# Layer 0's recurrence: one logistic operation per job, and half of the products with B on GpSimd

## The chip, the core and the metric

The kernel runs on one core of a Trainium2 chip. Its engines work from queues of their own and meet at semaphores: TensorE (PE in the rows; PEld is its weight load), VectorE (DVE), ScalarE (ACT), GpSimd (POOL) and SyncE (SP, which starts transfers). Each queue is strictly in order: an instruction that waits holds up all behind it. [...] The metric is the device time of one execution in microseconds (us), the median of several runs.

## The reference

The program is a tower of four layers over 32 images of 50 tokens with 192 features. The change lies in the mixer of layer 0, a bilinear state-space recurrence with 16 states per feature (shortened):

```python
A = -jnp.exp(A_log)                      # 192 features x 16 states
bc = x @ W_bc                            # B_sel, C_sel: 16 columns each
delta = softplus(x @ W_dt @ W_dtp + b_dt)
delta = soft_clamp(delta * rsqrt(mean(delta**2) + 1e-6) * rms_scale, 1e-4, 10.0)
half  = 0.5 * delta[..., None] * A
denom = 1.0 - half
A_bar = (1.0 + half) / denom
Bx    = sqrt(delta)[..., None] * B_sel[:, :, None, :] / denom * x_in[..., None]
h_t   = A_bar_t * h_{t-1} + Bx_t         # over the 50 tokens of an image
y     = sum over states of C_sel * h + D_param * x
```

With r = 1/denom, a number between 0 and 1, the decay A_bar is 2r - 1. denom is 1 + 0.5 exp(A_log) delta, so r is also the logistic function of -(ln delta + A_log - ln 2).

## The kernel before

The stage works on features in partitions and tokens along the free dimension. The 1600 tokens are cut into 4 chunks of 400, the turns of a loop (`CHUNKS`). The 192 x 16 pairs of feature and state are cut into 24 jobs a chunk (`JOBS0`): two jobs of three hold 128 features of one state, the third holds the remaining 64 features of two states, which two copies side by side fill to 128 rows. A job is thus 128 rows of 400 tokens, float32.

The work of a job j, in `bilinear_scan`, is shared out so:

- TensorE spreads the row of B over 128 partitions into a bank of PSUM (`spread_b`, line 558, two banks that alternate), does the same with C (`spread_c`, line 558), and adds the result of a job to the sum over states (`add`, line 575, with the identity, or with the folded identity for the third kind of job). Its order is spread_b(j+1), spread_c(j), add(j-2).
- ScalarE computes ln(1 + coef x rate) (`logarithm`, line 600), then its exponential with a minus sign, r (`invert`, line 607), then the decay 2r - 1 into PSUM (`decay`, line 613). Its order is logarithm(j), invert(j-1), decay(j-2). There are two buffers of decays, so that decay(j) waits for the scan of job j-2.
- GpSimd multiplies the input with r (line 633), into `w1`.
- VectorE multiplies `w1` with the spread row of B from PSUM (`weigh`, line 650, into `w2`), scans over the tokens (`recur`, line 656), and multiplies the states with the spread row of C (`read`, line 662). Its order is weigh(j), read(j-1), recur(j). At a chunk's end it writes y (line 675).

All this is written out by hand as the order of each engine's instructions; there is no planner. Four slots of each buffer (`SLOTS`) and semaphores that count jobs keep the engines apart. Ahead of the loop `split_thirds` splits B and C into three bfloat16 parts, on VectorE (lines 501 to 509), as a block of its own: blocks are parted by a barrier of all engines. Layer 3 has a scan of its own (`scan`, from line 680). There B's row goes from PSUM into SBUF on ScalarE (line 821) and GpSimd does the product with it (line 850); the lines 742 (add), 746 (spread), 805 (decay), 875 (scan) and 881 (read) belong to it.

The lines that set TensorE's order:

```python
spread_b(0)
for j in range(jobs):
    if j + 1 < jobs:
        spread_b(j + 1)
    spread_c(j)
    if j >= 2:
        add(j - 2)
```

The functions that the change touches, as they are before it:

Of the kernel before, what the change touches and what calls it, by code (L numbers as in the profile page):

```python
# [489 lines left out]
def split_thirds(t, bc, thirds, select, select_pair):  # L490

    nc = t.nc
    with ExitStack() as inner:
# [3 lines left out]
        with t.block() as block:  # L497
            @block.vector
# [22 lines left out]
def bilinear_scan(t, u, rate, coef, bc, direct, gain, y):  # L521
# [5 lines left out]
    jobs = JOBS0  # L527
    group = lambda j: job_states(j)[0]
    with ExitStack() as st:
# [3 lines left out]
        split_thirds(t, bc, thirds, select, select_pair)  # L533
        names = ("den_done", "r_done", "a_done", "w1_done", "w2_done", "s_done", "g_done", "summed", "b_spread", "c_spread", "y_done", "a_zero")
        (den_done, r_done, a_done, w1_done, w2_done, s_done, g_done, summed, b_spread, c_spread, y_done, a_zero) = (t.sem(n) for n in names)
        w2, s, g_, den, r, w1 = (t.sbuf(n, [128, SLOTS, CHUNK], st) for n in ("w2", "s", "g", "den", "r", "w1"))
# [7 lines left out]
        with t.block() as block:  # L544
            @block.tensor
            def _(pe):
                pe.sem_inc(summed, SLOTS)
                pe.wait_ge(fold_done, 1)
                with pe.Fori(0, CHUNKS) as c:
# [10 lines left out]
                    def spread_b(j):  # L560
                        pe.wait_ge(w2_done, c * jobs + j - 1 + SLOTS)
                        pe.sem_inc(t.passed, 1)
                        spread_row(bankB[j % 2], j, 0).then_inc(b_spread, 1)
# [61 lines left out]
            def _(pool):  # L625
                pool.sem_inc(w1_done, SLOTS)
# [1974 lines left out]
```

## Time and profile before

| what | value |
|---|---|
| median of 3 runs | 2521.09 us (2516.54 to 2526.69) |
| the profiled execution | 2526.45 us, its span 2524.6 us |
| TensorE busy | 2005.6 us, 79% of the span |
| VectorE busy | 1189.0 us, 47% |
| ScalarE busy | 890.3 us, 35% |
| GpSimd busy | 843.8 us, 33% |
| mean granted clock | 0.859 |

The shares are means over stages with different limits; layer 0's recurrence, from about 205 to 397 us, is one of them. The span is the time from the first to the last instruction of the one execution whose trace is read. In rows of the order of time the first two numbers are start and duration in us; the square brackets say how long the engine was idle before and what ended that. Durations of one engine's neighbours overlap a little, so that the distance from start to start is what an instruction costs its engine.

### The profile page before, as it was taken

To read this page: it belongs to the slowest core of one execution; us is meant where nothing else is said; L and a number is where in the kernel's file an instruction comes from. 1 tells how busy PE (TensorE), PEld (TensorE's weight loads), DVE (VectorE), ACT (ScalarE), POOL (GpSimd) and SP (SyncE) were. 2 spreads that over 40 slices of the span, in tenths; PEclk is the share of its full clock that TensorE was granted. 3 is DMA by queue.
4 is the path that set the end of the run, shared out by engine and by line. 5 is a ranking of instruction groups with operands and counts; after the bars stand their busy time and mean duration, and the time that the engine had idled before them with its cause. 6 is when DMAs were issued, how large, how long until landed. Compare 5 with 4: busy or idle time off the path is not lost. (4 is left out here: it accounts for less than half of the span.)

```text
span 2524.6 us, 42132 instructions
## 1 busy us (share of the span) xinstructions
PE 2005.6 (79%) x13338; PEld 1484.1 (59%) x13338; DVE 1189.0 (47%) x2907; ACT 890.3 (35%) x1860; POOL 843.8 (33%) x759
## 2 busy tenths in 40 slices
PE   9755777987995994985995567777499938999998
PEld 8511223665764883664983222224399837999987
DVE  4348995243563113563113799998222243222222
ACT  1247784133233332342224644553222122211211
POOL 0203552012111553001552267663234312443443
PEclk9757997876896995895997789999599957999999
DMA  7100000000004871003871000000377626777774
GB/s 217 31 0 1 0 0 1 0 0 6 1 0 122 237 206 35 1 0 106 225 205 26 0 1 0 0 0 1 113 223 221 170 69 191 224 222 224 221 201 113
DMA packets 95935, 228.18 MB, mean 90 GB/s; under 512 B 22481, under 2 KB 60948, under 8 KB 87540
## 3 DMA queue, kind: packets, MB, share of 16 engines
q1 hardware_dynamic: 64564, 188.81, 23.4%
q0 software_dynamic: 31296, 38.48, 8.4%
q8 instruction: 34, 0.56, 0.1%
q14 instruction: 41, 0.34, 0.0%
HBM read 199.63 MB, written 27.62 MB: 90 GB/s over the span
## 5 line engine op out<-in xcount | busy, mean ns | idle before, releaser
L1964 PE MATMUL banks<-wt,hid 128*128 128x192 f32 x1932 | 331.7, 327 | 0.4
L1964 PEld LDWEIGHTS banks<-wt,hid 128*128 128x128 f32 x1932 | 311.8, 190 | 1.5 <-issue 0.6
L1866 POOL DMA_INDIRECT xblock<-table,take x169 | 167.6, 992 | 370.7 <-DVE gate L2149 193.8
L1939 PE MATMUL banks<-xTblock,wt 128*128 128x256 f32 (+1 forms) x1464 | 268.6, 341 | 1.7 <-ACT xTblock L2022 1.2
L2162 DVE TENSOR_TENSOR hid<-sa,banks 128x512 f32<-128x512 f32 (+1 forms) x183 | 105.9, 579 | 340.1 <-ACT sa L2043 337.3
L2043 ACT ACTIVATE sa<-banks 128x512 f32<-128x512 f32 (+1 forms) x183 | 93.3, 510 | 481.5 <-PE banks L1950 476.6
L1939 PEld LDWEIGHTS banks<-xTblock,wt 128*128 128x128 f32 x1464 | 237.6, 194 | 23.7 <-issue 1.9
L742 PE MATMUL banks<-g,consts 128*128 128x400 f32 x384 | 184.7, 571 | 60.1 <-DVE g L881 56.1
L850 POOL TENSOR_TENSOR w<-u,spreadB 128x400 f32<-128x400 f32 x192 | 192.9, 1034 | 87.0 <-ACT spreadB L821 87.0
L1871 POOL DMA_INDIRECT sums<-yblock,put x96 | 152.7, 1591 | 170.5 <-issue 98.6
L875 DVE TENSOR_TENSOR_SCAN s<-banks,w 128x400 f32<-128x400 f32 x192 | 187.7, 977 | 4.2 <-POOL w L850 4.2
L2177 DVE TENSOR_SCALAR yblock<-banks,gate 128x192 f32<-128x192 f32 x129 | 49.4, 414 | 235.2 <-PE banks L1964 204.3
L742 PEld LDWEIGHTS banks<-g,consts 128*128 128x128 f32 x384 | 61.0, 197 | 168.4 <-DVE g L881 167.2
L633 POOL TENSOR_TENSOR w<-u,r 128x400 f32<-128x400 f32 x96 | 99.0, 1033 | 175.4 <-ACT r L607 163.4
L805 ACT ACTIVATE banks<-rate,coef 128x392 f32 x192 | 113.2, 591 | 117.8 <-DVE s L875 117.8
L1950 PE MATMUL banks<-xTblock,wt 64*128 64x256 f32 (+1 forms) x1464 | 143.3, 342 | 0.0
L1871 POOL DMA_INDIRECT out<-yblock,put x65 | 103.6, 1594 | 115.0 <-issue 56.5
L1950 PEld LDWEIGHTS banks<-xTblock,wt 64*128 64x128 f32 x1464 | 116.1, 187 | 22.9 <-issue 12.1
L881 DVE TENSOR_TENSOR g<-s,banks 128x400 f32<-128x400 f32 x192 | 103.3, 540 | 0.0
L1943 PE MATMUL banks<-xTblock,wt 128*128 128x256 f32 (+1 forms) x480 | 94.7, 349 | 2.2 <-ACT xTblock L2022 1.3
L656 DVE TENSOR_TENSOR_SCAN s<-banks,w 128x400 f32<-128x400 f32 x96 | 93.8, 977 | 0.1
L1926 PE MATMUL banks<-consts,xblock 128*128 128x128 f32 x338 | 61.5, 296 | 38.7 <-DMA xblock<-table,take 38.6
(379 smaller groups left out, 3455.5 us busy)
## 6 DMA issues: line engine op xcount, KB each, us to landing
wt<-L3f_packed SPq DMA_DIRECT2D x41, 1152.0 KB, 5.6
wt<-L_packed SPq DMA_DIRECT2D x60, 576.0 KB, 4.6
wt<-L3f_packed SPq DMA_DIRECT2D x41, 576.0 KB, 5.4
wt<-L3m_packed SPq DMA_DIRECT2D x20, 1152.0 KB, 5.4
wt<-L_packed SPq DMA_DIRECT2D x20, 675.0 KB, 4.2
wt<-L3m_packed SPq DMA_DIRECT2D x20, 577.0 KB, 5.4
pixels<-pixels SPq DMA_DIRECT2D x16, 375.0 KB, 4.8
wshift<-w_patch SPq DMA_DIRECT2D x8, 450.0 KB, 11.9
```

The source lines that it names most:

```text
L633: nc.gpsimd.tensor_tensor(w1[:, j % SLOTS, :], u[:, group(j), at], r[:, j % SLOTS, :], ALU.mult).then_inc(w1_done, 1)
L742: nc.tensor.matmul(acc[g][0:parts, 0:CHUNK], ident[0:parts, 0:parts], g_[:, j % SLOTS, :], start=(n == 0), stop=(n == STATES - 1)).then_in ...
L805: nc.scalar.activation(rest, rate[:, g, at].rearrange("p (b t) -> p b t", t=SEQ)[:, :, 1:SEQ], ACT.Exp, scale=coef[:, g, n:n + 1]).then_in ...
L850: nc.gpsimd.tensor_tensor(w2[:, j % SLOTS, :], u[:, g, at], spreadB[:, n % 2, :], ALU.mult).then_inc(bu_done, 1)
L875: nc.vector.tensor_tensor_scan(s[:, j % SLOTS, :], decays[j % DECAYS], w2[:, j % SLOTS, :], 0.0, ALU.mult, ALU.add).then_inc(s_done, 1)
L881: nc.vector.tensor_tensor(g_[:, j % SLOTS, :], s[:, j % SLOTS, :], bankC[(j // groups) % 2][0:parts, 0:CHUNK], ALU.mult).then_inc(g_done, 1)
L1866: nc.gpsimd.indirect_dma_start(x[:, b % 2, q - column_of_block[b], :], None, table, bass.IndirectOffsetOnAxis(take[:, q:q + 1], 0)).then_i ...
L1871: nc.gpsimd.indirect_dma_start(sums, bass.IndirectOffsetOnAxis(put[:, q:q + 1], 0), y[:, b % 2, q - column_of_block[b], :], None, compute_ ...
L1939: nc.tensor.matmul(bank[:, n * j:n * (j + 1)], wt[:, v, cols(base, 2 * p + j)], xT[:, v, 0, 0:n], start=(j == 0), stop=False, skip_group_c ...
L1950: last = nc.tensor.matmul(bank[:, n * j:n * (j + 1)], wt[half, v, cols(REST_AT, 2 * p + j)], xT[half, v, 1, 0:n], start=False, stop=True, ...
L1964: last = nc.tensor.matmul(bankY[s], hid[:, m, 128 * s:128 * (s + 1)], wt[:, v, DOWN_AT + DIM * m:DOWN_AT + DIM * (m + 1)], start=(m == 0 a ...
L2162: nc.vector.tensor_tensor(hid[:, 2 * p:2 * p + 2, 0:n], sa[:, (PAIRS * v + p) % 2, 0:2 * n].rearrange("p (m n) -> p m n", m=2), second[:, ...
```

## The change

Ahead of the loop, in the block of `split_thirds`, ScalarE replaces rate by its logarithm (four operations on 128 x 800). Per job, Ln and Exp are replaced by one logistic operation on that logarithm, with the scale -1 and a bias for each feature and state; `coef` now holds this bias, and the Exp that made `coef` is gone. The buffer `den` is gone. For odd jobs ScalarE copies the spread row of B from PSUM to SBUF (`spreadB`, two buffers), and GpSimd multiplies `w1` with it, behind the input's product of the next job. For even jobs VectorE multiplies as before. The semaphore `w2_done` becomes `even_weighed` and `odd_weighed`; `b_copied` counts the copies. TensorE's order is as before, but the spread of an odd row waits for the copy of the odd row before it.

```diff
+            @block.scalar
+            def _(act):
+                nc.scalar.preload_act_table_set("natural_log_exp_and_others")
+                for c in range(CHUNKS):
+                    at = slice(CHUNK * c, CHUNK * (c + 1))
+                    nc.scalar.activation(rate[:, :, at], rate[:, :, at], ACT.Ln)
+                nc.scalar.preload_act_table_set("sigmoid_and_others")
...
-                        pe.wait_ge(w2_done, c * jobs + j - 1 + SLOTS)
+                        if by_pool(j):
+                            pe.wait_ge(b_copied, c * HALVES + j // 2 + 1)
+                        else:
+                            pe.wait_ge(even_weighed, c * HALVES + j // 2 + SLOTS // 2)
...
-                for sem in (den_done, r_done, a_done):
+                for sem in (r_done, a_done):
                     act.sem_inc(sem, SLOTS)
-                nc.scalar.preload_act_table_set("natural_log_exp_and_others")
+                act.sem_inc(b_copied, 1)
...
-                    def logarithm(j):
-                        act.wait_ge(r_done, c * jobs + j + 1)
-                        act.sem_inc(t.passed, 1)
-                        nc.scalar.activation(den[:, j % SLOTS, :], rate[:, group(j), at], ACT.Ln,
-                                             scale=coef[:, j:j + 1], bias=1.0).then_inc(den_done, 1)
-
-                    def invert(j):
-                        act.wait_ge(den_done, c * jobs + j + 1 + SLOTS)
+                    def share(j):
                         act.wait_ge(a_done, c * jobs + j + 1)
                         act.wait_ge(w1_done, c * jobs + j + 1)
-                        nc.scalar.activation(r[:, j % SLOTS, :], den[:, j % SLOTS, :], ACT.Exp, scale=-1.0).then_inc(r_done, 1)
+                        act.sem_inc(t.passed, 1)
+                        nc.scalar.activation(r[:, j % SLOTS, :], rate[:, group(j), at], ACT.Sigmoid,
+                                             scale=-1.0, bias=coef[:, j:j + 1]).then_inc(r_done, 1)
+
+                    def copy_b(j):
+                        act.wait_ge(b_spread, c * jobs + j + 1)
+                        act.wait_ge(odd_weighed, c * HALVES + j // 2 + 1)
+                        nc.scalar.activation(spreadB[:, j // 2 % 2, :], bankB[j % 2][:, 0:CHUNK], ACT.Identity).then_inc(b_copied, 1)
...
-                            logarithm(j)
-                        if 0 < j <= jobs:
-                            invert(j - 1)
+                            share(j)
+                            if by_pool(j):
+                                copy_b(j)
...
-                    for j in range(jobs):
+
+                    def input_times_share(j):
...
+                    def weigh(j):
+                        pool.wait_ge(w1_done, c * jobs + j + 1 + SLOTS)
+                        pool.wait_ge(b_copied, c * HALVES + j // 2 + 2)
+                        pool.wait_ge(s_done, c * jobs + j + 1)
+                        nc.gpsimd.tensor_tensor(w2[:, j % SLOTS, :], w1[:, j % SLOTS, :], spreadB[:, j // 2 % 2, :],
+                                                ALU.mult).then_inc(odd_weighed, 1)
+
+                    for j in range(jobs + 1):
+                        if j < jobs:
+                            input_times_share(j)
+                        if j and by_pool(j - 1):
+                            weigh(j - 1)
...
-                        dve.wait_ge(w2_done, c * jobs + j + 1 + SLOTS)
+                        dve.wait_ge(odd_weighed if by_pool(j) else even_weighed, c * HALVES + j // 2 + 1 + SLOTS // 2)
...
-                        weigh(j)
+                        if not by_pool(j):
+                            weigh(j)
...
-                    nc.scalar.activation(coef[:], w["L0_A_job"], ACT.Exp).then_inc(coef_done, 1)
...
-                    dve.wait_ge(coef_done, 1)
-                    nc.vector.tensor_scalar(coef[:], coef[:], 0.5, None, ALU.mult)
+                    nc.vector.tensor_scalar(coef[:], w["L0_A_job"], -1.0, math.log(2.0), ALU.mult, ALU.add)
```

How the change moves instructions, engine by engine, in the middle of a chunk (the names in brackets are the semaphores that an instruction waits for; REGISTER_ALU is an instruction of the queue that only carries a wait or a count; `w_43` is `w2`, and `w_48` before or `w_47` after is `w1`). ScalarE before, one job:

```order
L613 ACTIVATE banks<-r,consts 128x8x49 [waits r_done_75,s_done_79]
L600 ACTIVATE den<-rate,coef 128x400 [waits r_done_75]
L604 REGISTER_ALU
L607 ACTIVATE r<-den 128x400 [waits w1_done_77,a_done_76,den_done_74]
L613 ACTIVATE banks<-r,consts 128x8x49 [waits r_done_75,s_done_79]
```

ScalarE after, an odd job and the even one behind it:

```order
L615 ACTIVATE r<-rate,coef 128x400 [waits a_done_75,w1_done_76]
L620 REGISTER_ALU [waits b_spread_82]
L621 ACTIVATE spreadB<-banks 128x400 [waits odd_weighed_78]
L625 REGISTER_ALU [waits s_done_79]
L627 ACTIVATE banks<-r,consts 128x8x49 [waits r_done_74]
L615 ACTIVATE r<-rate,coef 128x400 [waits a_done_75,w1_done_76]
L625 REGISTER_ALU [waits s_done_79]
L627 ACTIVATE banks<-r,consts 128x8x49 [waits r_done_74]
```

Two operations made r before; now one does. In the odd job the copy (L621), which waits for TensorE's spread, stands between r and the decay (L627).

TensorE before, two jobs:

```order
L558 MATMUL banks<-thirds,select 128x400 [waits w2_done_78]
L558 MATMUL banks<-thirds,select 128x400 [waits g_done_80]
L575 MATMUL banks<-g,consts 128x400 [waits g_done_80]
L561 REGISTER_ALU
L558 MATMUL banks<-thirds,select_pair 128x400 [waits w2_done_78]
L558 MATMUL banks<-thirds,select 128x400 [waits g_done_80]
L575 MATMUL banks<-g,fold 64x400 [waits g_done_80]
```

TensorE after, the same place:

```order
L569 MATMUL banks<-thirds,select 128x400 [waits even_weighed_77]
L580 REGISTER_ALU
L569 MATMUL banks<-thirds,select 128x400 [waits g_done_80]
L589 MATMUL banks<-g,consts 128x400 [waits g_done_80]
L569 MATMUL banks<-thirds,select_pair 128x400 [waits b_copied_73]
L580 REGISTER_ALU
L569 MATMUL banks<-thirds,select 128x400 [waits g_done_80]
L589 MATMUL banks<-g,fold 64x400 [waits g_done_80]
```

The order of the matmuls is the same: a spread of B, a spread of C, an add. What a spread of B waits for has changed, to `even_weighed` (VectorE's product) and `b_copied` (ScalarE's copy) in turn.

VectorE before, a scan and the whole job behind it:

```order
L656 SCALAR_TENSOR_TENSOR s<-banks,w_43 128x400 [waits a_done_76,w2_done_78]
L648 REGISTER_ALU [waits summed_81]
L650 TENSOR_TENSOR w_43<-w_48,banks 128x400 [waits b_spread_82,w1_done_77]
L662 TENSOR_TENSOR g<-s,banks 128x400 [waits c_spread_83,s_done_79]
L656 SCALAR_TENSOR_TENSOR s<-banks,w_43 128x400 [waits a_done_76,w2_done_78]
```

VectorE after, an even job and the odd one behind it:

```order
L683 TENSOR_TENSOR w_43<-w_47,banks 128x400 [waits b_spread_82,w1_done_76]
L695 TENSOR_TENSOR g<-s,banks 128x400 [waits c_spread_83,s_done_79]
L687 REGISTER_ALU
L689 SCALAR_TENSOR_TENSOR s<-banks,w_43 128x400 [waits a_done_75,even_weighed_77]
L695 TENSOR_TENSOR g<-s,banks 128x400 [waits c_spread_83,s_done_79,summed_81]
L688 REGISTER_ALU [waits odd_weighed_78]
L689 SCALAR_TENSOR_TENSOR s<-banks,w_43 128x400 [waits a_done_75]
```

The product is gone from the odd job: there the read of the even job stands right behind that job's scan, and the odd scan waits for GpSimd's product and ScalarE's decay.

## Rows read from the trace of the kernel before

**Rows 1.** busy us by engine in one stretch: us, PE, PEld, DVE, ACT, POOL, PEclk, DMA

```profile
252.00:300.00 48.00, 34.87 (x99) 11.15 (x97) 46.82 (x77) 38.67 (x76) 24.84 (x25) 0.96 0.00 0
```

**Rows 2.** order of time over one job, engines without weight loads

```profile
268.44 0.61 ACT L600 ACTIVATE den<-rate,coef 128x400 f32 x1
...
268.96 0.52 ACT L607 ACTIVATE r<-den 128x400 f32<-128x400 f32 x1
...
269.64 0.55 DVE L650 TENSOR_TENSOR w<-w,banks 128x400 f32<-128x400 f32 x1
269.68 1.03 POOL L633 TENSOR_TENSOR w<-u,r 128x400 f32<-128x400 f32 x1 [0.81 <-ACT r L607]
269.75 0.59 ACT L613 ACTIVATE banks<-r,consts 128x392 f32<-128x392 f32 x1 [0.28 <-DVE s L656]
270.10 0.56 DVE L662 TENSOR_TENSOR g<-s,banks 128x400 f32<-128x400 f32 x1
...
270.58 0.98 DVE L656 TENSOR_TENSOR_SCAN s<-banks,w 128x400 f32<-128x400 f32 x1
...
270.81 0.33 PE L558 MATMUL banks<-thirds,select_pair 96*128 x1 [0.15 <-DVE g L662]
...
270.98 0.83 PE L575 MATMUL banks<-g,consts 128*128 128x400 f32 x2
...
271.48 0.54 DVE L650 TENSOR_TENSOR w<-w,banks 128x400 f32<-128x400 f32 x1
```

**Rows 3.** order of time at the end of the first chunk, VectorE and TensorE

```profile
253.30 0.97 DVE L656 TENSOR_TENSOR_SCAN s<-banks,w 128x400 f32<-128x400 f32 x1
...
254.31 0.57 DVE L662 TENSOR_TENSOR g<-s,banks 128x400 f32<-128x400 f32 x1
...
254.93 0.89 PE L575 MATMUL banks<-g,fold 128*64 128x400 f32 x2 [0.56 <-DVE g L662]
...
255.75 0.68 PE L558 MATMUL banks<-thirds,select 96*128 x3
```

**Rows 4.** order of time in layer 3's scan

```profile
1502.42 0.94 PE L742 MATMUL banks<-g,consts 128*128 128x400 f32 x2 [0.42 <-DVE g L881]
...
1503.19 0.34 PE L746 MATMUL banks<-thirds,select 96*128 x1
...
1510.02 3.03 POOL L850 TENSOR_TENSOR w<-u,spreadB 128x400 f32<-128x400 f32 x3 [1.06 <-ACT spreadB L821]
...
1600.00 0.34 PE L746 MATMUL banks<-thirds,select 96*128 x1
...
1600.46 0.50 ACT L821 ACTIVATE spreadB<-banks 128x400 f32<-128x400 f32 x1 [4.44 <-PE banks L746]
1600.86 0.58 ACT L805 ACTIVATE banks<-rate,coef 128x392 f32 x1
```

**Rows 5.** order of time at the start of layer 0's recurrence, ScalarE

```profile
205.98 1.28 ACT L593 ACT_TABLE_LOAD   x1 [12.00 <-DVE banks L640]
...
208.33 0.52 ACT L607 ACTIVATE r<-den 128x400 f32<-128x400 f32 x1
```

**Rows 6.** order of time, a start of VectorE that ScalarE releases

```profile
160.55 0.87 ACT L981 ACTIVATE inv<-ln 128x800 f32<-128x800 f32 x1
...
161.45 0.99 DVE L1023 TENSOR_TENSOR d<-d,inv 128x800 f32<-128x800 f32 x1 [15.22 <-ACT inv L981]
```

**Rows 7.** order of time, TensorE at the granted clock 0.50

```profile
261.77 1.54 PE L575 MATMUL banks<-g,consts 128*128 128x400 f32 x2
...
263.10 0.54 PE L558 MATMUL banks<-thirds,select_pair 96*128 x1
```

**Rows 8.** busy us by stretch, columns as in the first group

```profile
252.00:261.50 9.50, 5.44 (x17) 1.59 (x15) 8.32 (x15) 7.16 (x15) 5.11 (x5) 1.00 0.00 1
262.00:265.00 3.00, 3.00 (x6) 0.60 (x5) 3.00 (x6) 2.45 (x6) 1.88 (x2) 0.50 0.00 0
266.00:276.00 10.00, 7.60 (x23) 2.33 (x21) 10.00 (x18) 8.56 (x17) 5.94 (x6) 1.00 0.00 0
```

More of the change, by code:

```diff
@@ L487, with split_thirds @@
 STATES = 16
-def split_thirds(t, bc, thirds, select, select_pair):
+def split_thirds(t, bc, thirds, select, select_pair, rate):
     nc = t.nc
@@ L527, in bilinear_scan @@
     jobs = JOBS0
+    HALVES = jobs // 2
+    by_pool = lambda j: j % 2 == 1
     group = lambda j: job_states(j)[0]
@@ L532, in bilinear_scan @@
         select_pair = t.sbuf("select_pair", [6 * STATES, STATES, 2, REST], st, BF16)
[L533 to L536, printed above, removed]
+        split_thirds(t, bc, thirds, select, select_pair, rate)
+        names = ("b_copied", "r_done", "a_done", "w1_done", "even_weighed", "odd_weighed", "s_done", "g_done", "summed", "b_spread", "c_spread", "y_done", "a_zero")
+        (b_copied, r_done, a_done, w1_done, even_weighed, odd_weighed, s_done, g_done, summed, b_spread, c_spread, y_done, a_zero) = (t.sem(n) for n in names)
+        w2, s, g_, r, w1 = (t.sbuf(n, [128, SLOTS, CHUNK], st) for n in ("w2", "s", "g", "r", "w1"))
+        spreadB = t.sbuf("spreadB", [128, 2, CHUNK], st)
         bankA, bankB, bankC, acc = t.bank[6:8], t.bank[0:2], t.bank[2:4], t.bank[4:6]
@@ L626, in _ @@
                 pool.sem_inc(w1_done, SLOTS)
+                pool.sem_inc(odd_weighed, SLOTS // 2)
                 with pool.Fori(0, CHUNKS) as c:
                     at = bass.ds(CHUNK * c, CHUNK)
-                    for j in range(jobs):
+                    def input_times_share(j):
                         pool.wait_ge(r_done, c * jobs + j + 1 + SLOTS)
-                        pool.wait_ge(w2_done, c * jobs + j + 1)
+                        if by_pool(j):
+                            pool.wait_ge(odd_weighed, c * HALVES + j // 2 + 1)
+                        else:
+                            pool.wait_ge(even_weighed, c * HALVES + j // 2 + 1)
                         pool.sem_inc(t.passed, 1)
@@ L640, in _ @@
                 nc.vector.memset(decays[1], 0.0).then_inc(a_zero, 1)
-                for sem in (w2_done, s_done, g_done):
+                dve.sem_inc(even_weighed, SLOTS // 2)
+                for sem in (s_done, g_done):
                     dve.sem_inc(sem, SLOTS)
@@ L650, in weigh @@
                         nc.vector.tensor_tensor(w2[:, j % SLOTS, :], w1[:, j % SLOTS, :], bankB[j % 2][:, 0:CHUNK],
-                                                ALU.mult).then_inc(w2_done, 1)
+                                                ALU.mult).then_inc(even_weighed, 1)
                     def recur(j):
-                        dve.wait_ge(w2_done, c * jobs + j + 1 + SLOTS)
+                        dve.wait_ge(odd_weighed if by_pool(j) else even_weighed, c * HALVES + j // 2 + 1 + SLOTS // 2)
                         dve.wait_ge(a_done, c * jobs + j + 1 + SLOTS)
@@ L922, in layer0_mixer @@
             names = ("mult", "low_done", "up", "mag_done", "exp_done", "max_done", "w_done", "d_done", "ln_done", "inv_done", "scaled_d",
-                     "merged", "soft", "squared", "meant", "logged", "rooted", "scaled", "tanh_done", "clamped", "root_done", "coef_done", "summed")
+                     "merged", "soft", "squared", "meant", "logged", "rooted", "scaled", "tanh_done", "clamped", "root_done", "summed")
             (mult, low_done, up, mag_done, exp_done, max_done, w_done, d_done, ln_done, inv_done, scaled_d,
-             merged, soft, squared, meant, logged, rooted, scaled, tanh_done, clamped, root_done, coef_done, summed) = (t.sem(n) for n in names)
+             merged, soft, squared, meant, logged, rooted, scaled, tanh_done, clamped, root_done, summed) = (t.sem(n) for n in names)
             bank_low, bank_up, bank_mean = t.bank[0:2], (t.bank[2:4], t.bank[4:6]), t.bank[6:8]
```

## The prediction

> **What bounds the kernel now.** The change touches one stage of some 190 us. I read it in this order: busy time by stretch (which engine is full), the order of time over one job (who waits for whom, and what each operation costs), the end of a chunk (what a missing cover costs), and layer 3's scan, which already has the copy and the GpSimd product that layer 0 now gets. In a chunk VectorE is busy 46.82 of 48 us, ScalarE 38.67, TensorE 34.87, GpSimd 24.84 [rows 1]. One job is 1.84 us from product to product (269.64 to 271.48) [rows 2], all of it VectorE, back to back: product with B 0.46 (start to start), read 0.48, scan 0.90. A pair of jobs is 3.69 us. Nobody makes VectorE wait: ScalarE's decay is ready two jobs ahead and itself waits 0.28 us for a scan; GpSimd waits 0.81 us for the share [rows 2]. So time is won only by taking work from VectorE, and lost by anything that makes a scan wait.
>
> **Removed from ScalarE**: Ln and Exp per job, 0.61 and 0.52 us [rows 2], 96 of each (24 jobs, 4 chunks); one logistic operation comes in. The trace has none; it lies between the Exp's 0.52 and the Ln's 0.61, both table operations on the same 128x400 operand, and I take 0.54 start to start. ScalarE is not the bound, so the difference is worth nothing in itself.
>
> **Removed from VectorE**: the product of the 48 odd jobs, 0.46 us each. But it stood between a scan and the read of the same scan. At a chunk's end, where nothing stands there, the read starts 1.01 us after the scan and not 0.90 (253.30 to 254.31) [rows 3]. So VectorE alone would need 3.69 - 0.46 + 0.11 = 3.34 us for a pair, 0.35 less.
>
> **Moved to GpSimd**: three products for a pair and not two. Three back to back take 3.03 us in layer 3 (1510.02) [rows 4]. That is under 3.34, so it costs nothing as long as each finds its operands; with the 0.20 us from ScalarE's end to GpSimd's start (269.48 to 269.68) [rows 2] before every one, 1.23 x 3 = 3.69 us is the other end. I take 3.03, the row of the same pattern.
>
> **Added before the loop**: four Ln over 128x800 and two table loads. ScalarE idled 12.00 us there [rows 5]. Four Ln at no more than twice 0.61 each, and two loads of 1.28, make 7.5 us: hidden. If that cover were gone it would be 7.5 us once. In return the loop's own load and first Ln go: the first share starts at 205.98 and not at 208.33, **-2.3 us** once [rows 5].
>
> **Added wait, and what is queued behind it.** This is where I put the result. ScalarE's order is now share(j), copy of B's row for odd j, decay(j-2), in one strict queue. The copy waits for TensorE's spread of that row. TensorE's order is unchanged: spread_b(j) stands behind spread_c(j-2) and add(j-4), and these two wait for read(j-4). In the kernel before only the product of job j itself wanted that row, and it came two jobs later. Now decay(j-2), needed by scan(j-2), stands behind it. With o = j-2: scan(o) waits for decay(o), that for the copy of row o+2, that for its spread, that for add(o-2), that for read(o-2), and this comes after scan(o-2). It is a ring that closes once per pair. Step by step, from one odd scan to the next:
> - scan to the next product 0.90, product to read 0.46 [rows 2];
> - read to TensorE's spread_c 0.71, that to the add 0.17 (270.10, 270.81, 270.98) [rows 2];
> - add to the spread behind it 0.77 with the identity (1502.42 to 1503.19) [rows 4], 0.82 with the folded one (254.93 to 255.75) [rows 3], one add in three: 0.79;
> - the spread itself 0.33; from its end to the copy's start 0.12 (1600.34 to 1600.46) [rows 4];
> - copy to the operation behind it 0.40 (1600.46 to 1600.86) [rows 4]; decay 0.59 [rows 2];
> - ScalarE's end to VectorE's start 0.03 (161.42 to 161.45) [rows 6].
>
> Sum 4.50 us against 3.69: **+0.81 us a pair**, with VectorE idle for 1.16. The copy's unknown is small: 0.40 to its full 0.50, 4 us in all.
>
> The ring is closed where an odd decay has a copy before it and an add of two jobs earlier: odd o from 3 to 21, ten pairs in a chunk, 40 in all. The other eight gain 0.35 each, 2.8 us. With TensorE at 2.4 GHz: 40 x 0.81 - 2.8 - 2.3 = **+27 us**.
>
> **TensorE's clock** now lies on the path. At 1.2 GHz the add holds the next spread 1.33 us and a spread takes 0.54 [rows 7]; spread_c to add is taken as twice 0.17. That adds 0.17 + 0.54 + 0.21 = 0.92, with the folded add somewhat more: 1.0 us. A pair is 5.50, and the sum 40 x 1.81 - 5.1 = **+67 us**. Which level? In the new ring at 2.4 GHz TensorE would be busy 0.33 for the even spread, 0.17 + 0.79 + 0.33 for the chain above, and 0.17 + 0.83 for the other job: 2.62 of 4.50 us, 58%. In the kernel before, it was busy 5.44 of 9.50 us, 57%, round a chunk's end at a granted clock of 1.00, and then stood at 0.50; there it was busy 3.00 of 3.00 and came back to 1.00, where it stayed at 76% [rows 8]. At 1.2 GHz the new ring would keep it busy 0.54, 0.34 + 1.36 + 0.54 and 0.34 + 1.54, some 4.7 of 5.5 us, 85%. So it would fall again and again and be raised again: I take half of the pairs at each level, 40 x 1.31 - 5.1 = **+47 us**.
>
> **Against the profiled execution**, 2526.45 us with a span of 2524.6, that gives 2573.8; it lay 5.4 above the median of the three runs, 2521.09. The forecast is for the median: 2521.1 + 47.3 = 2568.4.
>
> **The rivals.**
>
> *The clock stays at 2.4 GHz* in the ring: 2521.1 + 27.3 = 2548.4. For it: 57% alone did not lower the clock at once [rows 8]. Its longest TensorE pause is some 1.6 us, from the end of add(o+1) to the next even spread. [...] The trace speaks against it in one place: the 0.50 after 261.5 us follows a stretch at 57%, the share of the new ring [rows 8]. [...]
>
> *The clock stays at 1.2 GHz* nearly throughout, if 85% does not raise it: 2521.1 + 67 = 2588. For it: nothing in the rows rose from less than full activity.
>
> *VectorE's saving comes through* (the other side). If the copy never holds a decay up, a pair costs 3.34: -48 x 0.35 - 2.3 = -19.1, 2502.0. It needs the ring to close in 3.34 us, 1.16 less than its rows sum to; the single links carry 0.1 us of doubt each, not that much. It would hold if spread_b did not stand behind the add, which the order denies.
>
> *GpSimd sets the pace* at 3.69 a pair, every product waiting for ScalarE anew, with the ring no obstacle: no gain and no loss a pair, -2.3 in all, 2519. It would need the same 1.16 us to vanish from the ring.
>
> **How the numbers follow.** Alternating clock 50%, always high 19%, nearly always low 16%, VectorE's saving 8%, GpSimd's pace 7%. The likeliest gives 2568.4. The range leaves out the last two (15%) and little more: downwards the always-high case less 4 us for the handovers and 5 for the spread of runs, 2540; upwards the low case plus 4 for the copy and 5, 2597. About 0.5% (2508.5 to 2533.7) is what a measurement of this kernel can tell from no change: faster 0.08, same 0.07, slower 0.85.
>
> **What would show it.** Right: VectorE idle before every second scan for 1 us or more, released by ScalarE's decay; ScalarE idle before the copy, released by TensorE; a pair of jobs at 4.5 to 5.5 us; granted clock changing between 1.00 and 0.50 within the scan; the first product with B about 2 us earlier; no logistic time on the chain. Wrong: a pair at 3.34 us with VectorE full, or scans released by GpSimd's product; a logistic operation well over 0.6 us, or GpSimd's products over 1.1, would upset the prices, and table loads inside the loop the whole sum.

## The result, and the profile after

The changed kernel takes 2574.1 us (median of 4 runs, 2565.45 to 2583.65), the kernel before 2518.82 beside it (4 runs, 2515.87 to 2526.69). The ratio is 1.0215, with a 95% interval of 1.0193 to 1.0237: it is slower, by some 55 us. The forecast was 2568.4.

The profiled execution of after took 2568.29 us (span 2566.2). In it the stage, from the end of the second memset ahead of the loop to the end of the last y, runs from 205.55 to 450.54 us, 245.0 us. Before it ran from 205.74 to 397.46, 191.7 us. So the stage lost 53.3 us. The two profiled executions as wholes lie 41.8 apart: the rest lies in later stages that the change doesn't touch, and executions of either kernel differ by over 10 us among themselves. From here on stages are compared with stages.

The column PEclk of the views by stretch is the part of its full clock that TensorE was granted. The high clock is a granted clock of 1.00 here, the low clock one of 0.50; both stood in the kernel before, over 252 to 261.5 us and over 262 to 265 [rows 8]. They are what the prediction names 2.4 and 1.2 GHz. The traces show the granted part and no frequency.

What ends the idle time is read first. The view of the waits of after, 204 to 450 us, gives for each engine and line what it waited for: us in total, times, the longest.

```profile
ACT spreadB L621 <- PE banks L569: 112.2, 46, 4.7
DVE s L689 <- ACT banks L627: 61.7, 44, 2.2
PE banks L569 <- DVE w L683: 44.9, 42, 2.2
```

VectorE's scan (L689) now waits 61.7 us for ScalarE's decay (L627), in 44 of 96 scans; ScalarE's copy (L621) waits 112.2 us for TensorE's spread; the scan waits next to nothing for GpSimd (0.7 us in the grouped rows below). Before, VectorE did not wait for the decay at all: 46.82 of 48 us busy [rows 1], and it was the decay that waited for the scan [rows 2].

The grouped rows of after, 195 to 460 us (busy us, mean ns of one, and the idle time before them with its releasers):

```profile
L689 DVE TENSOR_TENSOR_SCAN s<-banks,w 128x400 f32<-128x400 f32 x96 | 94.7, 986 | 62.5 <-ACT banks L627 61.7 <-POOL w L659 0.7
...
L615 ACT ACTIVATE r<-rate,coef 128x400 f32 x96 | 58.8, 617 | 4.9 <-ACTq L606 4.8
...
L659 POOL TENSOR_TENSOR w<-w,spreadB 128x400 f32<-128x400 f32 x48 | 49.4, 1030 | 3.9 <-ACT spreadB L621 3.9
```

The logistic operation (L615) takes 617 ns, as the Ln did [rows 2]; GpSimd's product with B (L659) 1030 ns, as one of the three in [rows 4]. None of the new operations is dear; the time is in the waits.

The next rows are the order of time of after, without weight loads, over one ring: from an odd scan (226.69) to the next odd scan (231.08), with a mean granted clock of 0.89, and 1.00 over 227.60 to 230.60. Columns as in [rows 2].

```profile
226.69 0.99 DVE L689 TENSOR_TENSOR_SCAN s<-banks,w 128x400 f32<-128x400 f32 x1 [2.18 <-ACT banks L627]
...
227.60 0.55 DVE L683 TENSOR_TENSOR w<-w,banks 128x400 f32<-128x400 f32 x1
228.06 0.56 DVE L695 TENSOR_TENSOR g<-s,banks 128x400 f32<-128x400 f32 x1
...
228.54 0.98 DVE L689 TENSOR_TENSOR_SCAN s<-banks,w 128x400 f32<-128x400 f32 x1
...
228.77 0.33 PE L569 MATMUL banks<-thirds,select 96*128 x1 [0.15 <-DVE g L695]
...
228.94 0.84 PE L589 MATMUL banks<-g,consts 128*128 128x400 f32 x2
...
229.61 0.33 PE L569 MATMUL banks<-thirds,select_pair 96*128 x1
...
230.06 0.50 ACT L621 ACTIVATE spreadB<-banks 128x400 f32<-128x400 f32 x1 [1.83 <-PE banks L569]
...
230.46 0.59 ACT L627 ACTIVATE banks<-r,consts 128x392 f32<-128x392 f32 x1
...
231.08 0.99 DVE L689 TENSOR_TENSOR_SCAN s<-banks,w 128x400 f32<-128x400 f32 x1 [0.89 <-ACT banks L627]
```

They answer to [rows 2]. There, product follows product after 1.84 us and a pair of jobs takes 3.69; here a pair takes 4.39. The links that the prediction named follow each other without a gap: odd scan, product (227.60), read 228.06, TensorE's spread of C 228.77, add 228.94, spread of B 229.61, copy 230.06, decay 230.46, scan 231.08, which had waited 0.89 us. In between lies the even scan (228.54), which was ready and waits for nothing.

The same links at the low clock, in the ring that follows (granted clock 0.50 over 231.08 to 236.44):

```profile
233.15 0.49 PE L569 MATMUL banks<-thirds,select_pair 96*128 x1
...
233.44 1.54 PE L589 MATMUL banks<-g,consts 128*128 128x400 f32 x2
...
234.77 0.87 PE L569 MATMUL banks<-thirds,select 96*128 x2
...
235.43 0.50 ACT L621 ACTIVATE spreadB<-banks 128x400 f32<-128x400 f32 x1 [2.81 <-PE banks L569]
...
236.44 0.99 DVE L689 TENSOR_TENSOR_SCAN s<-banks,w 128x400 f32<-128x400 f32 x1 [1.87 <-ACT banks L627]
```

Here the pair takes 5.36 us (231.08 to 236.44). The add holds the next spread 1.33 us (233.44 to 234.77) and not 0.67.

The granted clock of after over 178 us of the scan, the last figure but two in the view by stretch (columns as in [rows 1]):

```profile
206.00:384.00 178.00, 130.58 (x280) 42.60 (x279) 121.93 (x180) 92.20 (x180) 108.25 (x108) 0.70 0.00 0
```

The same stretch of the kernel before:

```profile
206.00:384.00 178.00, 128.72 (x360) 42.38 (x358) 170.17 (x277) 145.84 (x280) 95.36 (x93) 0.94 0.00 0
```

The view of after in stretches of 4 us, two neighbours of them:

```profile
240.00:244.00 4.00, 2.18 (x8) 0.97 (x8) 2.83 (x5) 2.56 (x5) 2.37 (x4) 1.00 0.00 0
244.00:248.00 4.00, 3.28 (x8) 0.99 (x7) 3.11 (x5) 2.56 (x5) 2.62 (x3) 0.54 0.00 0
```

After 4 us at 1.00 in which TensorE was busy 2.18 us, the next 4 us had a mean of 0.54; over the whole stretch the mean is 0.70, where the kernel before had 0.94 in the same 178 us. In [rows 8] such a fall stood once, behind a chunk's end; now it comes again and again.

Last, the end of the first chunk in after, the counterpart of [rows 3]:

```profile
265.89 1.59 PE L589 MATMUL banks<-g,fold 128*64 128x400 f32 x2
...
267.42 1.04 PE L569 MATMUL banks<-thirds,select 96*128 x3
267.66 1.17 DVE L709 SCALAR_TENSOR_TENSOR rate<-xT,consts,banks 128x400 f32 x2 [1.82 <-PE banks L589]
...
268.39 0.50 ACT L621 ACTIVATE spreadB<-banks 128x400 f32<-128x400 f32 x1 [4.69 <-PE banks L569]
...
269.31 0.58 ACT L627 ACTIVATE banks<-r,consts 128x392 f32<-128x392 f32 x1
...
269.99 0.99 DVE L689 TENSOR_TENSOR_SCAN s<-banks,w 128x400 f32<-128x400 f32 x1 [0.69 <-ACT banks L627]
```

Here the prediction had seen nothing. The write of y (L709) waits 1.82 us for the last adds, 1.11 before, since they run at the low clock (0.50 over 265 to 268 us; 1.00 in the kernel before over 254 to 256.5). And the first scan of the next chunk (269.99) waits 0.69 us more for its decay (269.31), which stands behind the copy (268.39) of row 1, whose spread stands behind the last add of the chunk that ends. From the last scan to the next chunk's first it is 5.74 us (264.25 to 269.99), before 4.37.

### The profile page after: what moved, and what is told of

Its sections match the earlier page's. It is cut to its first block and busy times, and to the rows that moved or that the text cites. A ratio compares the mean times of both kernels' runs of the same rounds, so it can differ in the third digit from the quotient of the medians.

```text
span 2566.2 us, 42041 instructions
## 1 busy us (share of the span) xinstructions
PE 2043.4 (80%) x13338; PEld 1495.7 (58%) x13338; DVE 1174.6 (46%) x2859; ACT 867.7 (34%) x1816; POOL 888.9 (35%) x807
## 5 line engine op out<-in xcount | busy, mean ns | idle before, releaser
L652 POOL TENSOR_TENSOR w<-u,r 128x400 f32<-128x400 f32 x96 | 98.6, 1031 | 179.9 <-ACT r L615 176.6
L689 DVE TENSOR_TENSOR_SCAN s<-banks,w 128x400 f32<-128x400 f32 x96 | 94.7, 986 | 62.5 <-ACT banks L627 61.7
L569 PE MATMUL banks<-thirds,select 96*128 x128 | 52.1, 438 | 54.1 <-DVE w L683 25.3
```

Of the source, the lines that this page charges most:

```text
L652: nc.gpsimd.tensor_tensor(w1[:, j % SLOTS, :], u[:, group(j), at], r[:, j % SLOTS, :], ALU.mult).then_inc(w1_done, 1)
```

## The experiments

Each kernel is the changed one with the edit that its diff shows; the diffs of the last three are shortened. "Pair" is the distance from one odd scan to the next. The kernels of the copy behind the decay, of the early spreads and of either half alone ran beside 21 runs of the kernel before with a median of 2520.11 us; the other three, on another chip, beside 7 with 2515.51. The theory is the ring of the prediction; its rivals stand with each expectation.

### Opening the ring on ScalarE

The copy goes behind the decay, so that the decay no longer stands behind a wait for TensorE.

```diff
                         if j < jobs:
                             share(j)
-                            if by_pool(j):
-                                copy_b(j)
                         if j >= 2:
                             decay(j - 2)
+                        if j < jobs and by_pool(j):
+                            copy_b(j)
```

> The changed kernel with one thing moved: on ScalarE the copy of B's odd row stands behind decay(j-2) and not ahead of it. All is computed. The stage is counted from the end of the second memset to the end of the last write of y: 191.7 us in the kernel before, 245.0 in the changed one. THEORY (a ring through the copy ahead of the decay): no decay waits for a spread any more, VectorE sets the pace with the 3.41 us a pair that the changed kernel shows at its chunk ends, stage 48 x 0.28 + 2 = 15 us under the kernel before, about 176 to 180 us, run some 12 to 16 us faster than the kernel before; no scan waits for ScalarE's decay by more than 0.2 us. RIVAL 1 (the odd product is late for itself, wherever the copy stands: row, copy, product and scan in series): odd scans wait for GpSimd's product, stage 200 us or more, slower than the kernel before. RIVAL 2 (GpSimd's three products at 3.69 a pair): stage about 190, no difference.

Measured: 2511.5 us (10 runs), ratio to before 0.9975 (0.9951 to 0.9999); the stage 186.1 us. Nothing else was changed, and 59 of the 245 us are gone. The waits of this kernel, 206 to 440 us (a stretch that runs on into the next stages):

```profile
ACT spreadB L621 <- PE banks L569: 55.5, 42, 3.7
...
DVE s L689 <- ACT banks L627: 3.4, 7, 0.6
...
DVE s L689 <- POOL w L659: 2.8, 8, 0.8
```

ScalarE's copy still waits for its spread, 55.5 us, and the scan no longer for the decay: 3.4 us where it was 61.7. So the loss hangs on what is queued behind the copy, not on the copy's own wait. Most pairs take 3.41 us, every third 3.62, and one a chunk 4.3 to 4.7. That last one lies near a chunk's head: there the copy, which waited for its spread, holds up the share and the decay behind it, which are those of even jobs; the even scan waits 0.45 to 0.62 us for this decay, where at most 0.2 had been expected, and the odd one after it 0.26 to 0.52 for GpSimd's product. Of the 15 us that the theory gave for the stage 5.6 came. The longer pairs hold 6.8 of the rest, and the three turns from one chunk to the next, where decay(0) still stands behind the copy of row 1, another 1.2. The ring was the cause of the loss, but this order leaves a remainder.

### Opening it on TensorE

TensorE issues the spread of an odd row of B one job earlier, ahead of the spread of C and the add; ScalarE's order stays. The reader counts of `b_spread` are shifted to suit.

```diff
+                    spread_b(1)
                     spread_b(0)
                     for j in range(jobs):
-                        if j + 1 < jobs:
-                            spread_b(j + 1)
+                        if by_pool(j):
+                            for k in (j + 2, j + 1):
+                                if k < jobs:
+                                    spread_b(k)
                         spread_c(j)
```

> The changed kernel with its ScalarE order left alone (copy ahead of decay); only TensorE's order is changed: the spread of odd row j+2 is issued one place earlier, ahead of the spread of even row j+1 and of spread_c(j) and add(j-2), so that it stands behind add(j-3) and no longer behind add of the odd job whose successor waits. The counts that the readers wait for follow. All is computed. THEORY (ring): the copy then follows a read that is one job older; from scan(o-3) to scan(o) the chain is 1.01 + 0.71 + 0.17 + 0.79 + 0.33 + 0.12 + 0.40 + 0.59 + 0.03 = 4.15 us, and VectorE itself needs about 5.0 for these three jobs, so the ring no longer binds: stage 175 to 180 us, some 12 to 16 us faster than the kernel before, as in the run with the copy behind the decay. RIVAL (the copy's mere place and load on ScalarE cost the time, or GpSimd does): stage stays near 245.

Measured: 2506.14 us (6 runs), ratio 0.9938 (0.9919 to 0.9957); the stage 180.4 us. This is the best of all versions, 14 us under the kernel before and 68 under the changed one. Its scans, in the grouped rows of 195 to 400 us:

```profile
L692 DVE TENSOR_TENSOR_SCAN s<-banks,w 128x400 f32<-128x400 f32 x96 | 94.3, 982 | 3.5 <-ACT banks L630 2.0 <-POOL w L662 1.4
```

They waited 3.5 us in all, after 62.5. VectorE's order of time there over one pair, from an even scan to the next:

```profile
223.19 0.98 DVE L692 TENSOR_TENSOR_SCAN s<-banks,w 128x400 f32<-128x400 f32 x1
...
224.26 0.57 DVE L698 TENSOR_TENSOR g<-s,banks 128x400 f32<-128x400 f32 x1
...
224.75 0.98 DVE L692 TENSOR_TENSOR_SCAN s<-banks,w 128x400 f32<-128x400 f32 x1
...
226.59 0.98 DVE L692 TENSOR_TENSOR_SCAN s<-banks,w 128x400 f32<-128x400 f32 x1
```

A pair is 3.40 us, all VectorE: scan to the read that depends on it 1.07, read to scan 0.49, scan to product 0.90, product to read 0.46, read to scan 0.48. So the saving that the prediction priced at 0.35 a pair is there (0.28), once nothing stands in the ring. TensorE's granted clock is 0.92 over 206 to 384 us (0.70 in the changed kernel), with the same work per pair: the low clock was a consequence of the ring first, and then a part of its cost.

```profile
206.00:384.00 178.00, 134.56 (x384) 45.84 (x382) 164.09 (x246) 123.11 (x240) 144.11 (x144) 0.92 0.00 0
```

### Lengthening it

The copy is done twice, first into a buffer that nobody reads. If a pair is a ring through the copy, each gets longer by one copy, start to start, whatever the clock.

```diff
                         act.wait_ge(odd_weighed, c * HALVES + j // 2 + 1)
+                        nc.scalar.activation(spare[:, j // 2 % 2, :], bankB[j % 2][:, 0:CHUNK], ACT.Identity)
                         nc.scalar.activation(spreadB[:, j // 2 % 2, :], bankB[j % 2][:, 0:CHUNK], ACT.Identity).then_inc(b_copied, 1)
```

> The changed kernel with the copy of B's odd row done twice on ScalarE, the first time into a buffer that nobody reads; 0.40 us more of ScalarE per pair. All is computed. THEORY (the copy is a link of the ring): every linked pair is longer by 0.40, 4.79 us at the high clock and 5.77 at the low, stage 245 + 40 x 0.40 = 261, a few us more if the clock is low for longer; run 16 to 22 us slower than the changed kernel. RIVAL (ScalarE, busy some 2.9 us of 4.97 a pair, has the time, and something else sets the pace): stage 245.

Measured: 2593.59 us (4 runs), ratio 1.0314 (1.0292 to 1.0336); the stage 266.3 us. The rows of one ring of this kernel:

```profile
318.96 0.50 ACT L622 ACTIVATE spare<-banks 128x400 f32<-128x400 f32 x1 [1.83 <-PE banks L570]
...
319.36 0.50 ACT L623 ACTIVATE spreadB<-banks 128x400 f32<-128x400 f32 x1
...
319.74 0.60 ACT L629 ACTIVATE banks<-r,consts 128x392 f32<-128x392 f32 x1
...
320.37 0.99 DVE L691 TENSOR_TENSOR_SCAN s<-banks,w 128x400 f32<-128x400 f32 x1 [1.29 <-ACT banks L629]
```

The second copy takes 0.40 us from start to start, and the decay and the scan behind it come that much later. Pairs take 4.78 to 4.80 at a mean granted clock of 0.82 to 0.86 (six of them), and 5.76 or 5.77 at 0.50 to 0.70; in the changed kernel it was 4.39 and 5.37, so either kind is longer by 0.40. ScalarE has idle time in plenty (the copy had waited 1.83 us for the spread), and yet an added 0.40 us reaches the end in full: this is what being in the ring means. 40 x 0.40 makes 16 of the 21.3 us that the stage grew. The rest lies in the same 40 pairs, which take 220.3 us in all and 199.0 in the changed kernel: fewer of them are short (9 take 5.03 us or less, at a mean granted clock of 0.82 to 0.94, where 16 took 4.64 or less, at 0.82 to 1.00), and the clock over 206 to 384 us is 0.67, after 0.70.

### The clock by itself

TensorE gets four small products with zero more behind the add of every even job, added to a sum. They change nothing in the ring's order, and lie where TensorE would pause.

```diff
                         if j >= 2:
                             add(j - 2)
+                        if j >= 2 and not by_pool(j):
+                            for _ in range(4):
+                                nc.tensor.matmul(acc[0][:, 0:112], zero[:], w["ident"][:, 0:112], start=False, stop=False)
```

> The changed kernel, with four more matmuls (float32, 128x112, a zero weight, into the open sum of the first group) on TensorE behind the add of every even job, in the pause before the next even spread. They add nothing to the sum, stand behind all that the ring of the next odd scan wants, and keep TensorE busy where it had paused. All is computed. THEORY (the granted clock alternates because of these pauses, and its low level is worth 5.37 - 4.39 = 0.98 us a pair): granted clock at or near 1.00 through the stage, pairs at 4.39 with hardly one over 4.7; the 40 linked pairs averaged 4.97, so 40 x 0.58 = 23 us less, stage about 220, run some 20 to 25 us faster than the changed kernel, still some 30 slower than the kernel before. RIVAL (the 5.37 us has another cause than the clock, or more work on TensorE only lengthens the ring): stage 245 or more.

Measured: 2558.57 us (4 runs), ratio 1.0176 (1.0158 to 1.0193); the stage 225.1 us. Granted clock of this kernel by stretch, columns as in [rows 1]:

```profile
208.00:255.00 47.00, 37.98 (x158) 20.69 (x158) 34.07 (x50) 26.64 (x53) 31.74 (x33) 0.90 0.00 1
...
300.00:400.00 100.00, 77.02 (x336) 40.03 (x336) 77.30 (x114) 56.46 (x111) 66.07 (x67) 1.00 0.00 0
```

From 300 us on the clock stays at 1.00, and pairs take 4.39 us, or 4.63 where the folded add stands in them. Two pairs at the heads of the first two chunks (6.57 and 5.92) still met 0.50 (means 0.56 and 0.71). More work on TensorE made the stage 19.9 us shorter: that is what the low clock costs, and the other 33.4 us of the loss, 225.1 against 191.7, are left when it is nearly gone.

The first scan behind the end of the first chunk in this kernel, at a clock of 1.00:

```profile
266.19 0.99 DVE L694 TENSOR_TENSOR_SCAN s<-banks,w 128x400 f32<-128x400 f32 x1 [0.36 <-ACT banks L631]
```

It comes 4.70 us after the chunk's last scan (261.49), 5.74 in the changed kernel and 4.37 before. So the wait for the decay over the turn of the loop is there at the high clock too, but the larger part of what a chunk's end loses goes with the low one.

### Each half of the change alone

First the logistic operation alone: the Ln ahead of the loop and the share in one operation stay, all products go back to VectorE, and GpSimd's product with B and its semaphores are gone (not shown in the diff).

```diff
-                            if by_pool(j):
-                                copy_b(j)
...
-                        if not by_pool(j):
-                            weigh(j)
+                        weigh(j)
```

> Only the first half of the change: logistic on ln(rate), with all 24 products per chunk on VectorE and TensorE's waits as in the kernel before; no copy, nothing more on GpSimd. All is computed. THEORY: ScalarE was not the bound, so only the start is won: stage 191.7 - 2 = about 189.7, run 2 us faster, no measurable difference; per pair 3.69 as before. RIVAL (the logistic operation is dear, or ScalarE's share matters to the pace): stage off by 5 us or more either way.

Measured: 2515.99 us (10 runs), ratio 0.9977 (0.9962 to 0.9992); the stage 189.8 us. Pairs take 3.69 as before. The first product with B comes 2.6 us after the stage's start and not 4.5, which is the whole of the 1.9 us gained. The logistic half costs nothing and gives what the prediction booked for the start.

Then the product alone: Ln and Exp per job stay, the odd products go to GpSimd, with the copy ahead of the decay as in the change.

```diff
+                            logarithm(j)
+                        if 0 < j <= jobs:
+                            invert(j - 1)
-                            share(j)
-                            if by_pool(j):
-                                copy_b(j)
+                        if j < jobs and by_pool(j):
+                            copy_b(j)
                         if j >= 2:
                             decay(j - 2)
```

> Only the second half of the change: copy and GpSimd's odd product, with Ln and Exp per job as in the kernel before. ScalarE's order is logarithm(j), invert(j-1), copy of row j for odd j, decay(j-2). All is computed. THEORY: the ring is the same, since neither Ln nor Exp stands in it; a pair is 4.39 us at 2.4 GHz and 5.37 at 1.2 as in the changed kernel, stage 245 plus the 2 us of the start, about 247, run some 53 us slower than the kernel before. ScalarE's own work would be 2 x (0.54 + 0.44 + 0.53) + 0.40 = 3.42 us a pair, under both. RIVAL (ScalarE's load is what matters): longer than in the changed kernel by about 2 x 0.44 us a pair, 42 us, stage 285.

Measured: 2585.84 us (4 runs), ratio 1.0255 (1.0224 to 1.0287); the stage 258.6 us, 12 more than the theory gave with neither Ln nor Exp in the ring. Pairs of 5.37 us, as in the changed kernel, stand at a mean granted clock of 0.50 to 0.68; the four at 1.00 take 4.78 and not 4.39. One of these, from 298.27 to 303.05 with a granted clock of 1.00, in the order of time (L607 is the Ln, L614 the Exp, L652 the input's product, L659 the product with B):

```profile
297.25 0.50 ACT L619 ACTIVATE spreadB<-banks 128x400 f32<-128x400 f32 x1 [1.96 <-PE banks L561]
...
300.14 0.52 ACT L614 ACTIVATE r<-den 128x400 f32<-128x400 f32 x1
...
300.91 1.03 POOL L652 TENSOR_TENSOR w<-u,r 128x400 f32<-128x400 f32 x1 [0.47 <-ACT r L614]
...
301.90 1.03 POOL L659 TENSOR_TENSOR w<-w,spreadB 128x400 f32<-128x400 f32 x1
...
302.04 0.59 ACT L625 ACTIVATE banks<-r,consts 128x392 f32<-128x392 f32 x1
...
303.05 0.99 DVE L689 TENSOR_TENSOR_SCAN s<-banks,w 128x400 f32<-128x400 f32 x1 [1.29 <-POOL w L659]
```

The decay was done at 302.63 (302.04 and 0.59), and the scan starts at 303.05, when GpSimd's product has ended. That product stands in GpSimd's queue behind the input's product of the next job (300.91), which waited for the Exp (300.14), and the Exp stood at the end of an unbroken run of ScalarE from the copy at 297.25 on, which had waited for TensorE. So there is a second path, through GpSimd: 5.80 us from a copy (297.25) to the odd scan of the next pair. At the high clock it ends 0.40 behind the ring; at the low clock the ring hides it. Fourteen of the linked pairs take 4.78 to 4.84 us (mean granted clock 0.78 to 1.00); 14 x 0.40 is half of the 12 us. Another 3.8 lie in the three turns from one chunk to the next (8.73, 8.47 and 8.55 us from odd scan to odd scan, 7.63, 7.63 and 6.71 in the changed kernel), where the first odd scan waits 1.69 us for GpSimd's product. The rest was not split up. With the logistic operation r of a job is made one turn of ScalarE's loop earlier and in one operation, and there the scans waited 0.7 us for GpSimd in all.

Last, the product alone with TensorE's order of the second experiment, to see whether the logistic half is of use when the first ring is open.

```diff
+                    spread_b(1)
                     spread_b(0)
...
+                        if by_pool(j):
+                            for k in (j + 2, j + 1):
```

> Copy and GpSimd's odd product with Ln and Exp per job as in the kernel before, and TensorE's odd spreads issued one place earlier. All is computed. It asks whether the logistic half is needed once the ring is open. With the ring closed this kernel took 258.6 us for the stage, 4.79 a pair at the high clock, where odd scans waited for GpSimd's product behind a later Exp. THEORY: that second wait hangs on the decay that the copy held up, so it goes with the ring; ScalarE's own work is then 2 x (0.54 + 0.44 + 0.53) + 0.40 = 3.42 us a pair, as much as VectorE's 3.41, and a pair is 3.42 to 3.7: stage 182 to 193. RIVAL (Ln and Exp close a ring of their own through GpSimd's product): pairs stay at 4.4 or more, stage over 220.

Measured: 2537.89 us (4 runs), ratio 1.0077 (1.0051 to 1.0104); the stage 205.4 us, between what the theory and the rival gave. Most pairs go 3.41, 3.7 to 3.9, 4.79 in turn. The view by stretch of this kernel, columns as in [rows 1]:

```profile
208.00:255.00 47.00, 35.03 (x88) 12.01 (x89) 38.65 (x58) 40.01 (x84) 36.39 (x36) 0.79 0.00 1
```

ScalarE is busy 40.01 of 47 us here, 24.81 of the same 47 in the changed kernel. The order of time of one pair of 4.79, from 231.94 to 236.73 (L617 is the Exp, L655 the input's product, L662 the product with B, L628 the decay):

```profile
233.81 0.52 ACT L617 ACTIVATE r<-den 128x400 f32<-128x400 f32 x1
...
234.59 1.03 POOL L655 TENSOR_TENSOR w<-u,r 128x400 f32<-128x400 f32 x1 [0.47 <-ACT r L617]
234.62 0.58 ACT L628 ACTIVATE banks<-r,consts 128x392 f32<-128x392 f32 x1
...
235.58 1.03 POOL L662 TENSOR_TENSOR w<-w,spreadB 128x400 f32<-128x400 f32 x1
...
236.08 0.58 ACT L628 ACTIVATE banks<-r,consts 128x392 f32<-128x392 f32 x1
...
236.73 0.99 DVE L692 TENSOR_TENSOR_SCAN s<-banks,w 128x400 f32<-128x400 f32 x1 [1.29 <-ACT banks L628]
```

The scan's row names the decay (L628), but the one that ended last before it (236.08) is that of the next job: each scan has a decay of its own, the even scan at 233.79 must have used one before 234.62, and so 236.73 uses that of 234.62 at the latest. What was late is GpSimd's product, 235.58 to 236.61. It stood behind the input's product of 234.59, and that waited for the Exp of 233.81. ScalarE had worked without a pause from the copy at 230.93, which had waited 1.65 us for TensorE. It needs some 3.3 us a pair here (two jobs of Ln 0.52, Exp 0.42, decay 0.51, and a copy 0.40), with pairs of 3.41: it can't make up a delay. This is the second path again. The late spread stands behind a folded add at the low clock, here (228.77, 1.60 us, where one at the high clock takes 0.89) and in two more pairs of this kernel (240.85 and 291.58, 1.59 us each); the granted clock was 0.50 over 228.80 to 230.30, 240.85 to 242.30 and 291.58 to 293.00, and why was not settled. With the ring opened on TensorE, the logistic operation is worth 25 us of the stage (205.4 against 180.4), where alone it is worth 2.

## Why the prediction was right

**The ring.** It was the whole of the forecast, and it is there link by link. Taken and measured at the high clock, start to start: scan to product 0.90, measured 0.91; product to read 0.46, 0.46; read to the spread of C 0.71, 0.71; that to the add 0.17, 0.17; add to the spread of B 0.79, 0.67 with the identity; the spread and the handover 0.33 and 0.12, the same; copy 0.40, 0.40; decay and handover 0.62, 0.62. Sum 4.50, measured 4.39, or 4.63 with the folded add, one in three: 4.47 in the mean. For the low clock 5.50 was taken; it is 5.36 or 5.37 (mean granted clock 0.50 to 0.68), or 5.52 to 5.68 with the folded add (0.50 to 0.71). The sums are made for 2.4 and 1.2 GHz, which no run shows; the runs showed granted clocks of 1.00 and 0.50, at which an identity's add held the next spread 0.67 us (228.94 to 229.61) and 1.33 us (233.44 to 234.77).

**The clock.** Half of the pairs were put at each level. Of the 40 linked pairs 19 took 5.36 or more (mean granted clock 0.50 to 0.71), 16 took 4.64 or less (0.82 to 1.00), and 5 lie between (0.66 to 0.84). Together they take 198.99 us, 4.97 each where 5.00 was forecast. That the clock would fall and rise again was argued from rows; the half was a choice, which no row gave, and that it came so near is in part luck. The two rivals with one level throughout fall with that; the fourth experiment shows the time that the first of them meant, 225.1 us of stage where 191.7 + 27.3 = 219.0 was priced; its two pairs still at the low clock make 3.7 of the difference. That short pauses are enough for the fall was the author's estimate, from the 0.50 behind a stretch with TensorE busy 5.44 of 9.50 us [rows 8]. The longest pause of TensorE within the scan is 2.2 us in the view of waits, those in the rings shown are 1.07 at most, and the mean granted clock over 206 to 384 us was 0.70; with the pauses filled, in the fourth experiment, it was 0.96.

**The sum, stage against stage.** Forecast +47.3, measured +53.3. To the first odd scan: -2.3 forecast, -1.3 measured (7.00 to 5.70 us from the stage's start); the first product came 1.9 us earlier, counted like this (2.65, before 4.54), but the first odd scan waited 0.80 for a decay behind the copy. The 44 pairs within chunks: 40 x 1.31 - 4 x 0.35 = +51.0 forecast, +50.4 measured (162.25 to 212.63 us). Three chunk ends and the tail: -1.4 forecast, as the other four of the eight unlinked pairs, +4.2 measured (3.35 and 0.84).

**The step that failed** is "The other eight gain 0.35 each". Four do, at 3.41 us (0.28). The other four, where one chunk ends and the next begins, or the stage ends, lose, for two reasons. The ring closes there as well, since decay(0) stands behind the copy of row 1 and this row's spread behind the last add of the chunk before. And the last adds run at the low clock before y, at three of the four ends (the last folded add takes 1.59 us there, 0.50 granted, and 0.89 at the third chunk's end), which had been priced for the 40 linked pairs alone. The fourth experiment parts the two: at 1.00 its three turns take 6.58 to 6.59 us from odd scan to odd scan (before 6.20 to 6.22, after 7.63, 7.63 and 6.71), and its tail 3.85 (before 3.84, after 4.68). So of the 4.2 us lost 1.1 is the ring over the turn, and 3.1 the low clock. The condition "an odd decay with a copy before it" was too narrow: every decay behind a copy counts, also that of an even job over the turn of the loop. The step was 5.6 of the 6.0 us missing. The median lies 5.7 us over the forecast, inside what its range allowed.

**The smaller prices.** The logistic operation costs 0.52 us start to start (226.58 to 227.10 in after) with a duration of 0.617, as the Ln does; 0.54 was taken, and it is on no path. Three GpSimd products back to back take 3.01 us (207.13 in after), 3.03 was taken. The Ln ahead of the loop ended at 200.03 and its second table load at 201.31, beside VectorE's splitting that lasted until 204.13: hidden, as argued. VectorE alone needs 3.41 and not 3.34 for a pair, because the read behind a scan starts 1.07 us after it and not 1.01. GpSimd as the pace-setter, and VectorE's saving coming through, are excluded by 61.7 us of waits for the decay against 0.7 for GpSimd; the second experiment shows what the saving is worth when the ring is opened.

## What to carry to other kernels

When work is moved to another engine, look at what stands behind its new wait in that engine's queue, and follow that back to the engine that gained: if the way comes round to where it began, its links add up to a period, and idle time on any engine in it is no cover: here 0.40 us more on ScalarE, which had idled 1.83 us, made pairs of 4.39 and of 5.37 us 0.40 longer. Such a ring is opened by changing the order in one queue (an operand issued a turn earlier), which here turned 55 us lost into 14 won with the same operations. Look for it at the turn of the loop as well as in its middle, and read TensorE's granted clock beside it: here, with TensorE kept waiting in short pieces, it went from 0.94 to 0.70 over the same 178 us.

## What was not expected of the hardware

- The folded add costs the ring more than the identity's: from the spread of C to the folded add 0.26 us and from there to the next spread 0.82 (314.12, 314.38, 315.20 in after), with the identity 0.17 and 0.67 (228.77, 228.94, 229.61), both at a granted clock of 1.00. That is 0.24 us a pair where 0.05 between the two had been taken.
- From a scan to what stands behind it on VectorE is 0.90 us where that is a product (224.75 to 225.65 in the second experiment), 1.07 where it is the read of the scan's own result (223.19 to 224.26 there), and 1.01 for the same read in the last job of a chunk (264.25 to 265.26 in after). What makes the 0.06 between the last two was not looked into.
- Filling TensorE's pauses with products by zero raised its mean granted clock from 0.70 to 0.96 over 206 to 384 us, and so shortened the stage by 19.9 us, although TensorE had more to do.
